# Four gated transformer layers on one core: the expert router turned, scored and routed in one stage

## The reference, cut to what matters

```
x = x + tanh(g_ffn[2]) * L2_ffn(layernorm(x))

inh = sigmoid(x @ Wr / temperature)                       # 8 values per token
in_zone = (inh >= LOWER) & (inh <= UPPER)
dist = abs(inh - 1/e)
w = exp(-dist / 0.1) * in_zone
no_expert = w.sum(-1) < 1e-8
fb = exp(-dist / 0.3)
fb_w = fb where expert is one of the top 2 by fb, else 0   # ties: the lower index
fb_w = fb_w / clip(fb_w.sum(-1), 1e-8)
w = where(no_expert, fb_w, w)
w = w / clip(w.sum(-1), 1e-8)
out = sum over e of w[e] * (silu(x @ Wg[e]) * (x @ Wu[e])) @ Wd[e]
```

## Time and profile before

| | us |
|---|---|
| Median of 3 executions | 3735.12 (3733.15 to 3736.53) |
| Profiled execution, own time | 3736.7 |
| Its span, first to last instruction | 3734.9 |
| PE busy | 3185.8 (85%) |
| DVE busy | 2699.3 (72%) |
| ACT busy | 1695.1 (45%) |
| POOL busy | 1348.6 (36%) |
| TensorE clock granted, mean | 0.926 of full speed |

### The profile page before, as it was taken

The page is one execution under the profiler, slowest core; times in us unless marked ns, Lnnn a source line. Parts: engine busy times, 40 slices in busy tenths (PEclk is TensorE's granted clock), DMA queues, the critical chain, the costliest instruction groups (busy, mean ns, idle before and its releaser), DMA issues. The chain is left out here.

```text
span 3734.9 us, 91319 instructions
## 1 busy us (share of the span) xinstructions
PE 3185.8 (85%) x31627; PEld 2210.8 (59%) x31627; DVE 2699.3 (72%) x5527; ACT 1695.1 (45%) x3176; POOL 1348.6 (36%) x1624
## 2 busy tenths in 40 slices
PE   3687999999888795589967998679999788999978
PEld 1364787887666542456654665446666455666645
DVE  7666655555788779878867676879998556888755
ACT  1233223232777436655522222456666225666622
POOL 1665100000333100044410000369999107998822
PEclk8677999999899898789958999989999998999999
DMA  4311000000000005011210000300000100000011
GB/s 136 65 42 55 0 0 0 0 0 2 16 13 13 4 25 219 26 51 45 64 34 1 0 0 30 85 13 9 9 9 6 29 17 14 9 10 9 5 42 48
DMA packets 166506, 107.86 MB, mean 29 GB/s; under 512 B 91726, under 2 KB 153340, under 8 KB 165500
## 3 DMA queue, kind: packets, MB, share of 16 engines
q1 hardware_dynamic: 164812, 104.03, 9.7%
q10 hardware_dynamic: 1584, 2.44, 0.2%
HBM read 68.52 MB, written 16.78 MB: 23 GB/s over the span
## 5 line engine op out<-in xcount | busy, mean ns | idle before, releaser
L2499 POOL TENSOR_TENSOR la_turned<-la_turned,la_sines 128x1024 f32<-128x1024 f32 x128 | 302.2, 2361 | 121.1 <-DVE la_sines L2418 119.4
L2410 DVE TENSOR_TENSOR la_turned<-A,la_cos 128x1024 f32<-128x1024 f32 x128 | 156.7, 1224 | 130.2 <-ACT la_sq L2389 130.2
L2493 POOL TENSOR_TENSOR la_scaled<-la_turned,la_rlen 128x1024 f32<-128x1024 f32 x128 | 243.8, 1904 | 16.9 <-POOL la_rlen L2486 13.4
L1388 POOL COPY l1x_vd<-half 128x16 f32<-128x16 f32 x8 | 1.2, 213 | 490.9 <-POOLq L48 490.9
L916 PE MATMUL B<-l0f_mixed,l0f_sums 128*128 128x256 f32 x768 | 176.2, 379 | 0.0
L2800 ACT ACTIVATE gg_gate<-B,gg_b 128x512 f32<-128x512 f32 (+1 forms) x96 | 65.9, 686 | 211.6 <-PE B L2826 211.6
L2530 PEld LDWEIGHTS A<-ident,la_scaled 128*128 128x128 f32 x1024 | 120.5, 141 | 66.8 <-issue 66.5
L1719 POOL TENSOR_SCALAR l3x_factor<-l3x_raw 128x256 f32<-128x256 int32 x16 | 13.9, 871 | 398.4 <-DMA l3x_raw<-in_l3x_mask 397.2
L916 PEld LDWEIGHTS B<-l0f_mixed,l0f_sums 128*128 128x128 f32 x768 | 145.9, 190 | 19.8
L2545 PE MATMUL A<-la_wq,la_hT 128*128 128x512 f32 x256 | 148.0, 661 | 11.1 <-DVE la_sines L2418 11.1
L2423 DVE TENSOR_REDUCE la_length<-la_sq 128x16 f32<-128x1024 f32 x128 | 151.0, 1180 | 0.2 <-issue 0.2
(11 more groups left out here) (468 smaller groups left out, 9320.0 us busy)
## 6 DMA issues: line engine op xcount, KB each, us to landing
l1f_spill<-l1f_work SPq DMA_DIRECT2D x16, 768.0 KB, 3.3
l1f_xT<-l1f_spill SPq DMA_DIRECT2D x16, 768.0 KB, 6.0
l2x_ctx<-in_ctx SPq DMA_DIRECT2D x128, 64.0 KB, 2.2
memory_vd<-vd SPq DMA_DIRECT2D x64, 68.0 KB, 1.9
X<-in_x SPq DMA_DIRECT2D x4, 1024.0 KB, 11.1
gates_rows<-in_ctx_rows SPq DMA_DIRECT2D x16, 256.0 KB, 2.8
memory_ctxT<-in_ctxT SPq DMA_DIRECT2D x64, 64.0 KB, 1.9
l1x_ctxT<-in_ctxT SPq DMA_DIRECT2D x64, 64.0 KB, 1.8
```

The costliest lines, as they stand in the source:

```text
L2410: dve.tensor_tensor(heads(turned[j % 2][:]), made_heads, cos[:, :, None, :].broadcast_to([P, 2, HEADS3, W3]), ALU.mult)\
L2493: pool.tensor_tensor(by_head(scaled), by_head(turned), spread_heads(rlen[j % 2][:], W3), ALU.mult)\
L2499: pool.tensor_tensor(turned[j % 2][:], turned[j % 2][:], sines[j % 2][:], ALU.add)\
```

## The change

The three stages `l2f_in`, `l2f_turn` and `route` become one stage `route`, with all instructions written out instead of looped, and `feature_major` is removed.

- The six loads are issued in one go: three for the router (`router_in`), three for the experts (`experts_in`).
- POOL normalises all 16 chunks, each into its own buffer (`xn0` to `xn15`), with the instruction that DVE used (L200). DVE no longer does, and POOL no longer copies.
- PE turns chunk c + 1, then multiplies chunk c by the router weights. There are four PSUM banks for turned chunks and four for logits.
- ACT copies each bank straight to `l2f_xnT`. It sets its activation table at the start of the stage.
- DVE takes the logits from PSUM and scales them by 1 / temperature in one instruction (`keep`).
- The routing is done in three groups of chunks, 0 to 5, 6 to 11 and 12 to 15 (192, 192 and 128 columns), in two parts: `measure` up to the distance, `select` for the rest. Between them DVE keeps logits of later chunks. ACT takes a group's exponentials in its order of copies: the first behind the copy of chunk last + 1 (7 and 13), the two others behind the next copy.
- The two best experts are found by maxima (`choose_first`): maximum over the 8 values, mark the equal ones, multiply by 8, 7, ..., 1, take the maximum of that and mark it. It is done twice, with the first winner lowered by 2 in between. The division of the fallback weights by their own sum is left out, since the last division normalises them.

```diff
-    feature_major(nc, m, "l2f_turn", xnT, router=(wr, mix),
-                  prefetch=[(wg[:], d["l2f_wg"]), (wu[:], d["l2f_wu"]), (wd[:], d["l2f_wd"])])
+    with Stage(nc, "route") as st:
+        GROUPS = ((0, 6), (6, 12), (12, NCH))
...
+            @block.tensor
+            def _(pe):
+                def turn(c):
+                    pe.wait_ge(normed_x, c + 1)
+                    if c >= 4:
+                        pe.wait_ge(copied, c - 3)
+                    for t in range(TPC):
+                        last = pe.transpose(bank[c % 4][:, t * P:t * P + P], xn[c][:, t], m.ident[:])
+                    last.then_inc(turned, 1)
+
+                def route(c):
+                    pe.wait_ge(copied, c + 1)
+                    if c >= 4:
+                        pe.wait_ge(kept, c - 3)
+                    for t in range(TPC):
+                        last = pe.matmul(logits[c % 4][:, t], xnT[:, c * TPC + t], wr[:], start=True, stop=True)
+                    last.then_inc(routed, 1)
+
+                turn(0)
+                pe.wait_ge(router_in, 48)
+                for c in range(NCH):
+                    if c + 1 < NCH:
+                        turn(c + 1)
+                    route(c)
...
+                for c in range(NCH):
+                    copy_x(c)
+                    for g, (first, last) in enumerate(GROUPS):
+                        if c == last + 1:
+                            inhibit(g)
+                        if c == last + 2:
+                            weigh(g)
+                inhibit(2)
+                weigh(2)
...
+                def keep(c):
+                    dve.wait_ge(routed, c + 1)
+                    dve.tensor_scalar(flat(mix[:, c * TPC:c * TPC + TPC]), flat(logits[c % 4]), temp[:], None, ALU.mult)\
+                       .then_inc(kept, 1)
+
+                def measure(g):
+                    inh, mask, dist = group[g][:3]
+                    dve.wait_ge(kept, GROUPS[g][1])
+                    dve.sem_inc(scored[g], 1)
+                    dve.wait_ge(inhibited[g], 1)
...
+                def choose_first(g, fb, sel):
+
+                    key, peak = group[g][6], group[g][10]
+                    n = peak.shape[1]
+                    then(dve.tensor_reduce(peak[:], fb[:], AX, ALU.max))
+                    then(dve.tensor_tensor(key[:], fb[:], spread_heads(peak[:], E), ALU.is_equal))
+                    then(dve.tensor_tensor(key[:], key[:], descending[:, None, :].broadcast_to([P, n, E]), ALU.mult))
+                    then(dve.tensor_reduce(peak[:], key[:], AX, ALU.max))
+                    then(dve.tensor_tensor(sel[:], key[:], spread_heads(peak[:], E), ALU.is_equal))
+
+                def select(g):
+                    inh, mask, dist, w, fb, sel, key, total, none, some, peak = group[g]
+                    dve.wait_ge(weighed[g], 1)
+                    then(dve.tensor_tensor(flat(w[:]), flat(w[:]), flat(mask[:]), ALU.mult))
+                    then(dve.tensor_reduce(total[:], w[:], AX, ALU.add))
+                    dve.tensor_scalar(none[:], total[:], 1e-8, None, ALU.is_lt)
+                    dve.tensor_scalar(some[:], total[:], 1e-8, None, ALU.is_ge)
+                    choose_first(g, fb, sel)
+                    then(dve.scalar_tensor_tensor(flat(inh[:]), flat(sel[:]), -2.0, flat(fb[:]), ALU.mult, ALU.add))
+                    choose_first(g, inh, mask)
+                    then(dve.tensor_tensor(flat(sel[:]), flat(sel[:]), flat(mask[:]), ALU.add))
+                    then(dve.tensor_tensor(flat(fb[:]), flat(fb[:]), flat(sel[:]), ALU.mult))
+                    then(dve.tensor_tensor(fb[:], fb[:], spread_heads(none[:], E), ALU.mult))
+                    then(dve.tensor_tensor(w[:], w[:], spread_heads(some[:], E), ALU.mult))
+                    then(dve.tensor_tensor(flat(w[:]), flat(w[:]), flat(fb[:]), ALU.add))
+                    then(dve.tensor_reduce(total[:], w[:], AX, ALU.add))
+                    then(dve.tensor_scalar(total[:], total[:], 1e-8, None, ALU.max))
+                    then(dve.reciprocal(total[:], total[:]))
+                    then(dve.tensor_scalar(total[:], total[:], m.tanh_g[:, 6:7], None, ALU.mult))
+                    dve.tensor_tensor(mix[:, tiles_of(g)], w[:], spread_heads(total[:], E), ALU.mult)
...
+                for c in range(6):
+                    keep(c)
+                kept_between, kept_behind = ((6, 7), (12, 13), ()), ((8, 9, 10, 11), (14, 15), ())
+                for g in range(len(GROUPS)):
+                    measure(g)
+                    for c in kept_between[g]:
+                        keep(c)
+                    select(g)
+                    for c in kept_behind[g]:
+                        keep(c)
+
+            @block.gpsimd
+            def _(pool):
+                for c in range(NCH):
+                    normed_chunk(pool, m, xn[c], c * TPC).then_inc(normed_x, 1)
```

More of the change, by code:

```diff
@@ L702, in normed_chunk @@
     return last
[L705 to L787, removed]
@@ L1142, in _ @@
                 for tile, src in ((wr, "l2f_wr"), (temp, "l2f_temp"), (lower_e, "c_lower_e")):
-                    sp.dma_start(tile[:], d[src]).then_inc(loaded, 16)
-                sp.wait_ge(loaded, 48)
-    wg, wu, wd = (own.enter_context(nc.sbuf_tensor(f"l2f_{n}", [P, E, P], F32)) for n in ("wg", "wu", "wd"))
-    feature_major(nc, m, "l2f_turn", xnT, router=(wr, mix),
-                  prefetch=[(wg[:], d["l2f_wg"]), (wu[:], d["l2f_wu"]), (wd[:], d["l2f_wd"])])
[L1150 to L1156, removed]
+                    sp.dma_start(tile[:], d[src]).then_inc(router_in, 16)
@@ new lines, in _, with copy_x, inhibit, weigh @@
+            @block.scalar
+            def _(act):
+                def copy_x(c):
+                    act.wait_ge(turned, c + 1)
+                    act.copy(xnT[:, c * TPC:c * TPC + TPC].rearrange("p t k -> p (t k)"), bank[c % 4]).then_inc(copied, 1)
+                def inhibit(g):
+                    act.wait_ge(scored[g], 1)
+                    act.activation(group[g][0][:], mix[:, tiles_of(g)], ACT.Exp, scale=-1.0).then_inc(inhibited[g], 1)
+                def weigh(g):
+                    inh, mask, dist, w, fb = group[g][:5]
+                    act.wait_ge(measured[g], 1)
+                    act.activation(w[:], dist[:], ACT.Exp, scale=-10.0)
+                    act.activation(fb[:], dist[:], ACT.Exp, scale=-1.0 / 0.3).then_inc(weighed[g], 1)
+                act.preload_act_table_set("natural_log_exp_and_others")
+                for c in range(NCH):
+                    copy_x(c)
+                    for g, (first, last) in enumerate(GROUPS):
+                        if c == last + 1:
[4 more added lines that the diff above has]
+                weigh(2)
@@ L1174, in _ @@
[L1174 to L1194, removed]
@@ L1195, in _ @@
-                then(dve.tensor_tensor(w[:], w[:], spread_heads(some[:], E), ALU.mult))
-                then(dve.tensor_tensor(flat(w), flat(w), flat(fb), ALU.add))
-                then(dve.tensor_reduce(total[:], w[:], AX, ALU.add))
-                then(dve.tensor_scalar(total[:], total[:], 1e-8, None, ALU.max))
-                then(dve.reciprocal(total[:], total[:]))
-                then(dve.tensor_scalar(total[:], total[:], m.tanh_g[:, 6:7], None, ALU.mult))
-                dve.tensor_tensor(mix[:], w[:], spread_heads(total[:], E), ALU.mult)
```

50 lines of the change are left out of this document (32 added, 18 removed).

## The result

The changed kernel takes 3726.51 us (median of 20 executions, 3717.17 to 3872.4), the kernel before 3736.53 us (20 executions, 3731.96 to 3746.86). The ratio is 0.9968, 95% interval 0.9961 to 0.9975: 12 us faster, 9 to 15. Two of the 20 executions ran at a lower clock throughout (3871 us) and are left out of the ratio; the other 18 have a median of 3725.6 us. I had forecast 3710, a gain of 25 us, with a range up to 3724, so the result lies above the range and the gain is half of what I forecast.

What follows compares the result with a forecast made beforehand. PE, then DVE, bound one unoverlapped stretch of layer 2. With POOL keeping pace and routing overlapped in groups, its end moves from 1979.97 to 1954.8 us: gain 25.2 off the 3735.12 median, about 3710; range 3704 to 3724.

Steps and rivals of the forecast that it cites:

- What bounds the kernel: Layer 2, about 1893 to 1981 us: PE bounds turning and logits, then DVE the routing, nothing of the next part overlapping.
- Start of the stage: Three stages become one: POOL starts at about 1893.6 us; two barriers and the wait leave the path.
- GpSimd's normalisation: POOL's 64 instructions of 128x128 at 0.50 us each, with a gap of 0.06 to 0.07 between two.
- P: POOL's time to normalise one chunk of four instructions: 2.28 us, just under PE's 2.45.
- rival A: GpSimd is the bound: at 0.66 us an instruction gain 18 us, at 0.85 gain 8; chance 0.26.
- rival C: Slower than before: GpSimd's operation with pointer scalars costs over 1 us; at 1.2 us, 3746 us; chance 0.07.
- 14 P + 1920.2: Routing's end in us with POOL slow, set by chunk 13 and 24.6 us of DVE behind it.
- PE's period and clock: PE's transposes and logit products in the routing stage stay at 2.45 us a chunk, clock at 0.50.
- DVE's prices: Routing chain on DVE: measure 3.0 us (last group 2.4), select 8.95 (last 7.7), keep 0.25.
- The sum for a POOL in time: Routing's chain of waits with POOL keeping up with PE: last routing instruction ends at 1954.8 us, not 1979.97.
- Rival B: DVE and POOL shut each other out during first measure and select: end 8 us later, 3718 us; chance 0.08.
- The end of the sum: Whole kernel: gain of 25.2 us subtracted from the median of 3735.12, giving about 3710.

Runs made afterwards that it cites:

- experiment 2: Changed kernel with DVE normalising all 16 chunks (six first, then two behind each of five keeps), POOL idle there: 3712.77 us, ratio 0.9937 to the kernel before.
- experiment 3: Changed kernel with GpSimd's 64 normalisation instructions replaced by seven forms (constants, pointers, min/max, copy, tensor_tensor and so on) to price each: 3718.20 us, one execution.
- experiment 1: Changed kernel with DVE normalising chunks 0 to 5 and POOL only 6 to 15: 3714.45 us, ratio 0.9938 to the kernel before.
- experiment 5: Changed kernel with the two best experts found by comparing every pair again, per group, instead of by maxima: 3730.73 us, ratio 0.9976 to the kernel before.
- experiments 6 and 7: The kernel before and the changed kernel, each run once more unchanged for a second trace: 3737.86 and 3719.80 us, one execution each.
- experiment 8: Kernel with all normalisation on DVE, eight chunks first, regrouped as 0-4, 5-9, 10-15, ACT's exponential one chunk sooner: 3708.81 us, ratio 0.992 to the kernel before.

## Why the prediction was wrong

*What bounds the kernel:* right. The two stretches were bound by PE and then DVE, nothing overlapped them, and experiment 2's 28.5 us in the stretch came out as 23 us of the median (0.9919 to 0.9954, so 17 to 30).

*Start of the stage:* right. POOL began 0.73 us behind the reciprocal, as in my 1893.6, though the router's loads let DVE go only 2.6 us behind POOL's start, when it had nothing to do yet.

*GpSimd's normalisation:* the step that failed. I put it at 0.50 us with 0.07 between two, so P = 2.28; it is 0.787 us, each starts 0.775 us behind the one before, without a gap, and P = 3.10. I went by the row of the same shape and another operation (0.457) and said "a second operand to fetch". Experiment 3 shows what I should have read: the cost goes by the arithmetic. The add row, at 2.7 ns a column, gives 0.35 us for 128 columns before any fixed part, and 0.527 was measured for one multiply; the second operation adds 0.12 and the two pointers 0.145. The trace of the kernel before had more to go by, a multiply by a constant at two widths (the narrower one reads integers):

```profile
L1719 POOL TENSOR_SCALAR l3x_factor<-l3x_raw 128x256 f32<-128x256 int32 x16 | 13.9, 871 | 398.4 <-DMA l3x_raw<-in_l3x_mask 397.2
L898 POOL TENSOR_SCALAR l0f_sums<-early_h 128x512 f32<-128x512 f32 x2 | 3.0, 1496 | 0.2
```

A line through them gives an estimate of 0.56 us at 128 columns, and half of the difference between the 1.090 of the earlier trace rows and this 0.871 gives 0.11 for a second operation: 0.67 us without the pointers, where 0.642 was measured. I had 0.66 as an upper value in the sum, and gave rival A, at 0.66 and 0.85 us, a chance of 0.26.

*Rival A* happened. The formula under rival C, 14 P + 1920.2, gives 1963.6 at P = 3.10, a gain of 16.4 us; the stretch gained 15.6. So the chain of waits was right, and one size in it was not.

*PE's period and clock:* right where its input came in time (2.45 us at 0.50, experiments 1 and 2).

*DVE's prices:* right. Select 8.8 us undisturbed (8.95 predicted), 7.4 for the last group (7.7), measure 3.0 and 2.4, keep 0.25. The sum for a POOL in time, 61.2 us from the first normalisation, came out as 57.9 in experiment 1. Of the 3.3 us, 2.0 stand before the first measure (19.5 instead of 21.5 us), because DVE had the first chunks ready sooner than a POOL at 0.57 us an instruction; the rest is a DVE chain slightly cheaper than priced.

*Rival B (contention):* small here, and I gave it 0.08 for 8 us. Beside POOL the first select took 9.45 us instead of 8.8 and the chunks came every 3.25 to 3.4 us instead of 3.1, so chunk 13, which sets the second measure, came 0.8 us late. It need not be small: in experiment 5 instructions of the same kind, eight times as wide, made two chunks 5.3 us late, and in experiment 3 a tensor_tensor on POOL held a DVE instruction for 3.11 us.

The Trainium skill (GPSIMD Engine Reference, 4.1 Engine selection) has one-input work on GpSimd at roughly line rate. That fits copy and min/max (0.29 us) and not arithmetic by scalars (0.53 to 0.79 us). Its sentence ahead of section 1 has VectorE roughly twice as fast for elementwise arithmetic. For the duration of one normalisation the traces come near it, 0.34 us on DVE in experiment 2 and 2.3 times that on POOL; by the time from one start to the next, which is what a chunk costs, it is 0.26 against 0.775 us, 3 times. The shared interfaces of its section 1, with contention for VectorE instructions that have two SBUF inputs, agree with experiment 5.

*The end of the sum:* the median gained 12 us and the stretch 15.6; experiments 6 and 7 leave that to the scatter of the other layers, without settling it. POOL's price alone doesn't carry the result out of my range: 3735.12, the median that I started from, less 15.6 is 3719.5, inside it. Up to 3725.6 there are 6 us more: the median of before came out 1.4 us higher in 20 executions than in three, and 4 to 5 us lie outside the stretch, their cause open. I had no term for how far the rest of the kernel moves between executions.

## What to carry to other kernels

Price a moved instruction by rows of the same operation, and if the engine has none, by the nearest arithmetic rather than the nearest shape; then ask from which price on the engine becomes the pace of the whole pipeline, because the loss is multiplied by every chunk. Work moved off an engine to relieve it is only worth moving if that engine was late: here VectorE waited for TensorE all along, and giving the normalisation back to it nearly doubled the gain (28.5 us of the stretch instead of 15.6). An instruction in a queue that other work shares (ACT's exponentials between its copies) should be placed where its wait is over when it is reached: in experiment 8 it was moved ahead of the logits it needs, and ACT stood for 3.89 us.

## What was new of the hardware

- GpSimd's tensor_scalar on 128x128 f32 costs 293 ns for min and max, 527 for one multiply, 642 for subtract and multiply, and about 75 more for each pointer operand (experiment 3).
- Four VectorE instructions in a row with two inputs of 1536 columns (1.76 us undisturbed, mostly 1.89 beside POOL) slow GpSimd to less than half its pace: in experiment 5 a chunk came after 7.0 us instead of 3.1. A select of instructions of 192 columns (0.36 us, some 0.49) costs it 5 to 10% (3.25 to 3.4 us a chunk).
- Eight GpSimd tensor_tensor instructions in a row on 128x128 f32 held one VectorE tensor_scalar of 192 columns for 3.11 us instead of 0.26 (experiment 3, seen once); beside GpSimd's tensor_scalar the same instruction took 0.35 and 0.41 us.
- The part of the kernel that no edit touched differed by 10 us between two executions of one program, with the granted clock at 0.94 instead of 1.00 in layer 1's attention; the edited stretch repeated within 0.1 us. For effects below 0.3% the stretch in the trace tells more than the median.
